# Windowed attention of a 192-slot loop: two value stationaries per head, one score stationary for the first 64 queries

## The reference

```python
for i in range(DEPTH):                      # 6
    x = attn_layer(shift_tokens(x), Wqkv[i], q_scale[i], k_scale[i], Wo[i]) + x
    x = ffn_layer(shift_tokens(x), ln_g[i], ln_b[i], W1[i], b1[i], W2[i], b2[i]) + x
# attn_layer: 16 heads of 64, q and k normalised, scaled and rotated, then
bq = q.reshape(b, h, nw, 32, d)             # nw = 4 blocks of 32 queries
bk2, bv2 = look(bk), look(bv)               # keys/values of the block before and of the own block
mask = (it < jb) | (it > jb + 32) | (jb == -1)
sim = einsum('bhwie,bhwje->bhwij', bq, bk2) * 8.0
out = einsum('bhwij,bhwje->bhwie', softmax(where(mask, -max, sim)), bv2)
```

## Time and profile before

| | |
|---|---|
| device time, median of 3 runs | 3308.11 us (3307.62 to 3310.73) |
| span of the profiled execution | 3304.7 us |
| PE / PEld busy | 3125.4 us (95%) / 2192.5 us (66%) |
| DVE, ACT, POOL busy | 2884.0 (87%), 2663.4 (81%), 2447.9 (74%) |

### The profile page before, as it was taken

The page is one execution under the profiler, slowest core; times in us unless marked ns, Lnnn a source line. Parts: engine busy times, 40 slices in busy tenths (PEclk is TensorE's granted clock), DMA queues, the critical chain, the costliest instruction groups (busy, mean ns, idle before and its releaser), DMA issues.

```text
span 3304.7 us, 181505 instructions
## 1 busy us (share of the span) xinstructions
PE 3125.4 (95%) x71268; PEld 2192.5 (66%) x71268; DVE 2884.0 (87%) x6045; ACT 2663.4 (81%) x5440; POOL 2447.9 (74%) x2673
## 2 busy tenths in 40 slices
PE   6776899999999999999999999999999999999996
PEld 4443567676667676676767667676676767667665
DVE  7886789999899999899999899998899999899984
ACT  6886678888788888788888788888788888788874
POOL 3333778888788888788888778787787878788883
PEclk9988999999999999999999999999999999999997
DMA  3000112122222222222222212122221212212121
GB/s 79 8 7 10 47 51 59 50 59 71 67 56 53 56 53 77 63 54 55 54 55 74 68 50 59 50 59 77 57 59 50 59 50 77 66 50 59 50 58 50
DMA packets 150374, 182.24 MB, mean 55 GB/s; under 512 B 51572, under 2 KB 74162, under 8 KB 149554
## 3 DMA queue, kind: packets, MB, share of 16 engines
q1 hardware_dynamic: 150322, 181.55, 21.2%
HBM read 21.32 MB, written 2.10 MB: 7 GB/s over the span
## 4 chain that ended last, share of the span: by engine, by line
PE 57%; issue 13%; DVE 10%; ACT 10%; POOL 5%; SPq 1%; DVEq 1%; DMA 1%; ACTq 1%; POOLq 0%
PE bank L1252 13%; PE bank L1339 8%; PE bank L1322 7%; PE bank L1262 5%; PE bank L1363 5%; PE bank L1270 3%; PE bank L1290 3%; ACT L798 3%; DVE tb L966 3%; ACT P L774 3%; PE bank L1392 2%; ACT gl L766 2%; POOL qk L524 2%; DVE bank L1075 2%; PE bank L1400 2%
## 5 line engine op out<-in xcount | busy, mean ns | idle before, releaser
L533 POOL TENSOR_TENSOR qk<-qk,rn 128x512 f32<-128x512 f32 x768 | 803.0, 1046 | 356.8 <-DVE rn L985 356.8
L524 POOL TENSOR_TENSOR qk<-ta,tb 128x512 f32<-128x512 f32 x768 | 978.6, 1274 | 2.5 <-DVE tb L966 2.5
L1252 PE MATMUL bank<-wqkv,zsT 128*128 128x512 f32 x1536 | 819.9, 617 | 25.4 <-ACT vt L705 12.3
L963 DVE TENSOR_TENSOR ta<-bank,rot 128x512 f32<-128x512 f32 x768 | 527.5, 687 | 116.1 <-ACT sq L688 87.4
L966 DVE TENSOR_TENSOR tb<-bank,rot 128x512 f32<-128x512 f32 x768 | 523.0, 681 | 0.0
L1068 DVE TENSOR_REDUCE bank<-sq 128x32 f32<-128x2048 f32 x192 | 440.6, 2295 | 25.1
L688 ACT ACTIVATE sq<-bank 128x512 f32<-128x512 f32 x768 | 445.2, 611 | 14.8 <-PE bank L1252 12.1
L696 ACT ACTIVATE qkT<-bank 128x512 f32<-128x512 f32 x768 | 396.6, 602 | 57.1 <-PE bank L1290 56.9
L1363 PEld LDWEIGHTS bank<-wo,oT 128*128 128x128 f32 x3072 | 375.4, 193 | 92.4 <-issue 92.4
L743 ACT ACTIVATE znT<-bank,small 128x128 f32<-128x128 f32 x192 | 87.9, 458 | 431.8 <-PE bank L1383 431.8
L564 POOL TENSOR_TENSOR P<-P,rowsum 128x512 f32<-128x512 f32 x384 | 392.9, 1045 | 20.0 <-DVE rowsum L1083 20.0
(11 more groups left out here) (131 smaller groups left out, 5740.6 us busy)
## 6 DMA issues: line engine op xcount, KB each, us to landing
vs<-vt SPq DMA_DIRECT2D x1152, 128.0 KB, 2.4
wqkv<-L_ffn_Wqkv SPq DMA_DIRECT2D x6, 1024.0 KB, 5.0
zm<-zm SPq DMA_DIRECT2D x192, 31.8 KB
wqkv<-L_ffn_Wqkv SPq DMA_DIRECT2D x6, 512.0 KB, 3.7
wo<-L_ffn_Wo SPq DMA_DIRECT2D x6, 512.0 KB, 4.0
z_sb<-x SPq DMA_DIRECT2D x4, 512.0 KB, 5.1
ctxb<-ctx SPq DMA_DIRECT2D x32, 64.0 KB, 1.8
w<-L_ffn_W SPq DMA_DIRECT2D x6, 341.0 KB
```

The source lines that it names most:

```text
L524: g.tensor_tensor(o, i0, i1, ALU.add).then_inc(s["g_add"], 1)
L533: g.tensor_tensor(q3, q3, r3, ALU.mult).then_inc(s["g_qk"], 1)
L963: v_.tensor_tensor(ta[:, c].rearrange("p (h d) -> p h d", d=DH), bank[j % 2][:, :].rearrange("p (h d) -> p h d", d=DH), rot[:, o:o + 64].u ...
L1252: t_.matmul(bank[j % 2][:, :], zsT[:, pu, :], wqkv[:, 512 * j:512 * j + 512], start=True, stop=True).then_inc(s["p_qk"], 1)
```

## The change

`scores` and `attend` are regrouped. The first 64 queries (blocks 0 and 1, which use the same 64 keys) are scored with one stationary of 64 columns instead of two of 32, after all products of blocks 2 and 3. Block 2 (queries 64-95, keys 32-95) gets its two key blocks in swapped order, and its mask too. `vs` holds two value windows instead of three, keys 0-63 and 64-127, made by four DMAs instead of six. The swapped block then has its key block 1 on the partitions where window 0 holds block 1, and its key block 2 where window 1 holds block 2: its weights are copied twice, once into `PTA` with the block-2 half multiplied by zero and once into `PTC` with the block-1 half multiplied by zero (a scale per partition out of the constants), and window 0 and window 1 add up in PSUM. `attend` runs all of window 0 (96 moving columns: queries 0-95), then all of window 1 (64 columns: queries 64-127).

```diff
-                    for j in range(3):
-                        sp.dma_start(vs[rows, par, j, :], vt[32 * j:32 * j + 64, par, r, :]).then_inc(s[f"l_v{par}"], 16)
+                    for j in range(2):
+                        sp.dma_start(vs[rows, par, j, :], vt[64 * j:64 * j + 64, par, r, :]).then_inc(s[f"l_v{par}"], 16)
...
-                        a_.activation(PT[:, :, 64 * j:64 * j + 64],
-                                      bank[4 + j][:, :].rearrange("p (h q) -> p h q", h=PAIRS),
-                                      ACT.Copy).then_inc(s["a_PT"], 1)
+                        pt = bank[4 + j][:, :].rearrange("p (h q) -> p h q", h=PAIRS)
+                        if j == 0:
+                            a_.activation(PTA[:, :, 0:64], pt, ACT.Copy).then_inc(s["a_PT"], 1)
+                        else:
+                            a_.activation(PTA[:, :, 64:96], pt[:, :, 0:32], ACT.Copy,
+                                          scale=cst[:, C_HALF:C_HALF + 1])
+                            a_.activation(PTC[:, :, 0:32], pt[:, :, 0:32], ACT.Copy,
+                                          scale=cst[:, C_HALF + 1:C_HALF + 2])
+                            a_.activation(PTC[:, :, 32:64], pt[:, :, 32:64], ACT.Copy).then_inc(s["a_PT"], 1)
...
                                 i = 32 * min(w, 1)
+                                o = 64 if w == 2 else 0
                                 t_.matmul(SC[e][32 * w:32 * w + 32, :], selb[dr, i:i + 32],
-                                          maskb[dr, :].unsqueeze(1).to_broadcast([64, PAIRS, DH]),
+                                          maskb[dr, o:o + 64].unsqueeze(1).to_broadcast([64, PAIRS, DH]),
                                           start=True, stop=False, skip_group_check=True)
                         for p in range(PAIRS):
-                            for w in range(4):
+                            for w in range(2, 4):
                                 for e in range(2):
                                     dr = slice(64 * e, 64 * e + 64)
-                                    k0 = WIN * max(w - 1, 0)
-                                    ins = t_.matmul(SC[e][32 * w:32 * w + 32, 64 * p:64 * p + 64],
-                                                    qkT[dr, p, 32 * w:32 * w + 32], qkT[dr, PAIRS + p, k0:k0 + 64],
-                                                    start=False, stop=p == PAIRS - 1, skip_group_check=True)
+                                    kb = qkT[dr, PAIRS + p, 32 * w - 32:32 * w + 32].rearrange("p (t c) -> p t c", t=2)
+                                    t_.matmul(SC[e][32 * w:32 * w + 32, 64 * p:64 * p + 64],
+                                              qkT[dr, p, 32 * w:32 * w + 32], kb[:, ::-1, :] if w == 2 else kb,
+                                              start=False, stop=p == PAIRS - 1, skip_group_check=True)
+                        for p in range(PAIRS):
+                            for e in range(2):
+                                dr = slice(64 * e, 64 * e + 64)
+                                ins = t_.matmul(SC[e][0:64, 64 * p:64 * p + 64], qkT[dr, p, 0:64],
+                                                qkT[dr, PAIRS + p, 0:64],
+                                                start=False, stop=p == PAIRS - 1, skip_group_check=True)
                         ins.then_inc(s["p_S"], 1)
...
-                        for i in range(4):
-                            for w, (q0, nq) in enumerate(((0, 64), (64, 32), (96, 32))):
+                        for w, (pt, q0, nq) in enumerate(((PTA, 0, 96), (PTC, 64, 64))):
+                            for i in range(4):
                                 for r in range(2):
                                     for e in range(2):
                                         kr = slice(64 * r, 64 * r + 64)
                                         hc = 128 * i + 64 * e
                                         ins = t_.matmul(bank[4 + r][64 * e:64 * e + 64, 128 * i + q0:128 * i + q0 + nq],
-                                                        vs[kr, pc, w, hc:hc + 64], PT[kr, 4 * e + i, q0:q0 + nq],
-                                                        start=True, stop=True)
-                            if i % 2 == 1:
-                                ins.then_inc(s["p_AV"], 1)
+                                                        vs[kr, pc, w, hc:hc + 64], pt[kr, 4 * e + i, :],
+                                                        start=w == 0 and i == 0, stop=w == 1, skip_group_check=True)
+                                if w == 1 and i % 2 == 1:
+                                    ins.then_inc(s["p_AV"], 1)
```

More of the change, by code:

```diff
@@ L42 @@
 MASKED = -(2.0 ** 120)
-C_ID, C_SH, C_TRI, C_ROT, C_MASK, C_SEL, C_BLK, C_END = 0, 128, 256, 384, 640, 704, 768, 772
+C_ID, C_SH, C_TRI, C_ROT, C_MASK, C_SEL, C_BLK, C_HALF, C_END = 0, 128, 256, 384, 640, 768, 832, 836, 838
 def constants():
@@ L71, in constants @@
     c[:, C_MASK:C_MASK + 64] = np.concatenate([first, later, first, later], 0)
+    c[:, C_MASK + 64:C_MASK + 96] = c[:, C_MASK + 32:C_MASK + 64]
+    c[:, C_MASK + 96:C_MASK + 128] = c[:, C_MASK:C_MASK + 32]
+    c[:, C_HALF] = (r // WIN) % 2
+    c[:, C_HALF + 1] = 1 - (r // WIN) % 2
     for i in range(4):
@@ L96, in build @@
         selb = sb("selb", [128, 64], BF16)
-        maskb = sb("maskb", [128, 64], BF16)
+        maskb = sb("maskb", [128, 128], BF16)
         z_sb = sb("z_sb", [128, B * E])
@@ L126, in build @@
         rowsum = sb("rowsum", [128, HEADS])
-        PT = sb("PT", [128, PAIRS, S])
+        PTA = sb("PTA", [128, PAIRS, 3 * WIN])
+        PTC = sb("PTC", [128, PAIRS, 2 * WIN])
         vt = sb("vt", [128, 2, 2, INNER // 2])
-        vs = sb("vs", [128, 2, 3, INNER // 2])
+        vs = sb("vs", [128, 2, 2, INNER // 2])
         oT = sb("oT", [128, PAIRS, S])
@@ L703, in copy_v @@
                         wait(act, "p_v", count(2, u, e + 1))
-                        wait(act, f"l_v{pu}", 96 * ((u - 2) // 2) + 96 if isinstance(u, int) else (u >> 1) * 96)
+                        wait(act, f"l_v{pu}", 64 * ((u - 2) // 2) + 64 if isinstance(u, int) else (u >> 1) * 64)
                         a_.activation(vt[:, pu, e, :], bank[e][:, :], ACT.Copy).then_inc(s["a_v"], 1)
@@ L808, in _ @@
             v_.tensor_copy(selb[:, :], cst[:, C_SEL:C_SEL + 64]).then_inc(s["u_bf"], 1)
-            v_.tensor_copy(maskb[:, :], cst[:, C_MASK:C_MASK + 64]).then_inc(s["u_bf"], 1)
+            v_.tensor_copy(maskb[:, :], cst[:, C_MASK:C_MASK + 128]).then_inc(s["u_bf"], 1)
             dve.wait_ge(s["u_dmc"], 1)
@@ L1329, in attend @@
                     if c_on:
-                        wait(pe, f"l_v{pc}", 96 * (c // 2) + 96 if isinstance(c, int) else (c >> 1) * 96 + 96)
+                        wait(pe, f"l_v{pc}", 64 * (c // 2) + 64 if isinstance(c, int) else (c >> 1) * 64 + 64)
                         wait(pe, "a_PT", count(2, c, 2))
                         pe.nop(nofuse=True)
-                        for i in range(4):
-                            for w, (q0, nq) in enumerate(((0, 64), (64, 32), (96, 32))):
+                        for w, (pt, q0, nq) in enumerate(((PTA, 0, 96), (PTC, 64, 64))):
+                            for i in range(4):
                                 for r in range(2):
```

## The result

The changed kernel takes 3326.24 us (median of 4 runs, 3324.66 to 3329.8) beside 3307.86 for the kernel before: a ratio of 1.0061, 95% interval 1.0046 to 1.0075. It is slower, as forecast, but by 18 us and not by 65. Its profiled execution has a span of 3327.7, 23.0 above that of before; it is the slowest of the four, so the traces lie some 5 us further apart than the medians.

A forecast was written before the change was run, and what follows sets the result against it. The prediction took a chain of waits through PE, ACT and DVE as the bound. Scores +0.60 and attend -0.25 gave +0.35 us a slot, +67 over 192 slots, net +65: 3373 us, own range 3345 to 3430, wider 3300 to 3430.

The forecast's parts named there:

- mixed circle: Chain of waits through PE, ACT and DVE, once round per slot of 15.06 us; score and attend changes go straight in.
- Steps 1 to 3: Scores: two halves of 16 rounds plus a tile-shape switch, 2.00 us against 1.40, +0.60 us a slot.
- step 1: Scores of blocks 2 and 3: 64 matmuls on four tiles, 16 rounds of 58 ns, 0.93 us.
- Step 4: Attend: 8 rounds at 85 ns and 8 at 58, 1.14 us against 1.40, -0.25 us a slot.
- Step 5: ACT's copies of P: 1.59 us, +0.50, covered by longer scores; otherwise attend waits 0.13, up to 0.2 us.
- Step 6: DVE readers of the scores: scores end some 0.6 us later, still ahead of rowmax, so covered.
- Step 7: Two fewer of six DMAs per unit on SP's queue, taken as 0; constants under 0.4 us, once.
- 192 slots: +67: Whole kernel: the sum of +0.35 us a slot, taken over 192 slots, gives +67 us.
- some 2: Slots at layer changes, where PE waits for zn anyway: takes back some 2 us of the loss.
- A: Rival, scores and attend: time follows the number of matmuls; -0.3 us a slot, about 3250 us; chance 0.11.
- B: Rival: scores no longer, attend's 0.25 gain lost waiting for copies of P; -0.05 a slot, about 3300 us; chance 0.07.
- C: Rival, scores and attend: loads not hidden or rounds keep 78 ns; +1.0 us a slot, 3500 us; chance 0.08.

The follow-up runs named there:

- e4: The kernel before with the change's new score grouping alone, old attend, three value windows and six DMAs; 3385.11 us, ratio 1.0234.
- e3: The changed kernel with the old grouping of the scores, keeping new attend, new copies of P and four DMAs; 3284.15 us, ratio 0.9931.
- e8: The changed kernel with two plain copies of the second half of P instead of three, nothing zeroed; 3327.66 us, ratio 1.0064.
- e1: The changed kernel with six DMAs per unit again, the third value window going to a tile nobody reads; 3336.67 us, ratio 1.0085.
- e2: The kernel before with four DMAs instead of six, block 2's values not the right ones; 3297.56 us, ratio 0.9973.
- e9: The changed kernel with four more slots written out as straight code ahead of the loop; 3325.41 us, ratio 1.0039.
- e5: The kernel before with four more slots written out as straight code ahead of the loop; 3308.21 us, ratio 1.0005.
- e6: The changed kernel with the merged first-64 products inside the loop over head pairs, switching tile shape for each pair; 3691.21 us, ratio 1.1161.

## Why the prediction was right or wrong

- **Direction and mechanism: right.** The mixed circle sets the slot; scores and `attend` lie in it. e4, with the scores alone, lengthens the slot by what the stage grows (0.52 and 0.53). PE's waits ahead of `transpose_qk` and in `proj_qk(3)` stayed: these stages take 1.12 and 2.16 us from start to start in both kernels.
- **Steps 1 to 3, scores: right in kind, too large.** +0.60 forecast, +0.53 measured (e4). The change of shape inside the stage is there (0.99 less 16 x 56 ns leaves 0.09), but the gap of 0.06 to 0.16 forecast ahead of `attend` is not: `attend` has the same tile shape as the merged scores, its copies of P are ready, and its first matmuls go in between their last. Rounds took 56 ns in step 1, not 58. That is 0.07 us a slot, 13 us of the miss. The whole looped slot grew by 0.27 where the sum had 0.35.
- **Step 4, attend: right.** -0.25 forecast, 1.29 against 1.53 in e3, rounds of 85 ns with 96 columns.
- **Step 5, copies: right.** 1.60 us against 1.59; covered (e8). That `attend` would wait 0.13 to 0.2 if scores didn't grow was too small: e3 showed it starting 0.27 later.
- **Step 6, DVE: right.** `rowmax` starts as long after the mask as before.
- **Step 7, DMAs: wrong.** "Nothing waits there in a normal slot; taken as 0" was true of a normal slot only. They are worth 10 us at the layer changes (e1, e2).
- **The sum was the larger error, and the step that failed.** "192 slots: +67", less "some 2" at layer changes, took every slot for a looped one, although the mean slot of the kernel before, (3262.9 - 346.4) / 191 = 15.27 us between the first and the last mask, is 0.24 above the looped 15.03. Those 45.6 us of excess were to be seen before, in slots whose length another wait sets. The term of 2 us measured 29: 15 at the layer changes and 15 in the first and last slots. Together with the 15 us by which the looped slots were overrated that is the miss of 42 us between 65 and 23 (47 between the medians).
- **What the 15 us at layer changes are.** 7.7 are shorter waits for `zn`, nearly all by the DMAs (7.2); the longer slot as such takes little off them (17.9 against 18.4 in e1; 15.2 in e4, whose slot is 0.52 longer), as the prediction's "some 2" had it. The rest goes with the granted clock, which the prediction took as full all along. It is also most of what lies between the kernel before and e1, 30.4 and 25.3 us with nearly the same waits: three slots at 0.83 or 0.84 before, none in e1. Why it falls less deep after the change was not tried.
- **What the 15 us in the first and last slots are.** The excess there falls from 15.2 to 0.6 us. Some 5 of it are the lower clock of slots 1 and 188, which stayed at 1.00 in e2: the chance of one execution, as far as these traces tell. The rest are the stops of code that runs for the first time (e9 against e5), less of them with fewer instructions and in a slot with more room; how these two share it isn't settled.
- **The number.** 3326 lies below the forecast's own range of 3345 to 3430. That it lies within the wider 3300 to 3430 is owed to terms that the prediction did not have.
- **Rivals.** A (time follows the number of matmuls) is wrong for a looped slot by e4; as a mechanism it has, by inference, a place in code that runs for the first time. B didn't come for the changed kernel, and is what e3's looped slot does: the wait for the copies takes back what `attend` gains. C, hidden loads failing, did not come.

## What to carry to other kernels

Merging two small stationaries into a wider one halves the instructions and not the time when the tiles ran side by side: count rounds (matmuls on the same tile, one after another), not matmuls, and take the loads as one bound and the moving columns as the other. Here the merge of the value windows paid and the merge of the scores didn't; doing only the first gave 0.9931 of the time. And before a loss or gain per slot is multiplied by the number of slots, compare the mean slot with the looped one: what lies between them has another cause, and moves by itself. Read the granted clock by slot there, not by slice of the page.

## What the runs showed of the hardware that was not expected

- Going from 64x32 to 64x64 tiles and back costs 0.14 us each way (e6), as much as two and a half rounds; in the changed kernel the matmuls of `attend` follow the merged scores, of the same tile shape, with no gap.
- With 224 matmuls in the two stages, the same slot takes 1.0 to 3.0 us longer the first time its code runs, in straight code and in the first pass of a loop alike (before and e5), with stops of 0.8 to 1.9 us in which PE issues nothing.
- A DMA issue holds SP's queue 0.6 us, and two of them, hidden in a looped slot, cost 10 us over five layer changes: 7 as waits of PE and the rest with the clock that falls behind such a wait.
- A slot in which PE waited 1.9 to 3.8 us for `zn` lost another 1.1 to 2.5 us where the granted clock fell (0.83 to 0.92 in the slot), and 0.2 where it did not.
